# A pairwise-interaction tower in native fp32 row tiles, with half of the groups turned so that the batch lies on the partitions

## What is computed

```python
e = jnp.stack([tbl_0[ids[:, 0]], ..., tbl_31[ids[:, 31]]], axis=1)   # 1024 x 32 x 64
xi, xj = e[:, idx_i, :], e[:, idx_j, :]                              # i < j, 496 pairs
z = jnp.sum(jnp.einsum('bpd,pde->bpe', xi, W) * xj, axis=-1)         # 1024 x 496
h = jnp.concatenate([z, dense_ctx], axis=1)                          # 1024 x 512
h = jnp.maximum(h @ W_top1 + b_top1, 0.0)
h = jnp.maximum(h @ W_top2 + b_top2, 0.0)
y = h @ W_top3
```

## Time and profile before

| | us |
|---|---|
| median of 3 runs (lowest, highest) | 643.97 (643.26, 646.44) |
| span of the profiled execution | 631.3 |
| median less span | 12.7 |
| PE busy | 515.1 (82%) |
| PE weight loads busy | 260.2 (41%) |
| DVE busy | 390.0 (62%) |
| ACT busy | 220.5 (35%) |
| POOL busy | 344.0 (55%) |
| mean granted TensorE clock | 0.935 of full |

### The profile page before, as it was taken

One profiled execution on the slowest core, in us unless ns is written; L12 is line 12 of the kernel. 1 busy time (PEld: TensorE's weight loads), 2 busy tenths in 40 slices (PEclk: granted clock), 3 DMA queues, 4 the chain that ended last, 5 costly groups with the idle time before them and its releaser, 6 DMA issues.

```text
span 631.3 us, 6463 instructions
## 1 busy us (share of the span) xinstructions
PE 515.1 (82%) x2288; PEld 260.2 (41%) x2288; DVE 390.0 (62%) x408; ACT 220.5 (35%) x387; POOL 344.0 (55%) x346
## 2 busy tenths in 40 slices
PE   1324028698899979999993999699799999999998
PEld 0112014244454435455551454344355555555542
DVE  1221026688799976877773135597678887877720
ACT  1621125344443425325142244254344433332003
POOL 7777727466444347678474445658788844332000
PEclk9997558799899999999997899899899999999999
DMA  2131102222322242331110000122223331110000
GB/s 38 34 75 43 27 20 52 43 56 57 58 58 50 53 108 42 65 71 23 29 23 19 18 15 20 37 61 59 54 41 62 67 58 31 35 29 2 1 0 0
DMA packets 72453, 25.77 MB, mean 41 GB/s; under 512 B 67555, under 2 KB 68067, under 8 KB 72421
## 3 DMA queue, kind: packets, MB, share of 16 engines
q1 hardware_dynamic: 63908, 15.91, 13.4%
q0 software_dynamic: 8512, 9.45, 7.3%
HBM read 25.34 MB, written 0.00 MB: 40 GB/s over the span
## 4 chain that ended last, share of the span: by engine, by line
PE 72%; another core or an unknown queue 8%; issue 7%; DVE 5%; POOL 4%; ACT 2%; DMA 1%; DVEq 0%; ACTq 0%
PE z_sum L628 24%; PE left L610 20%; PE left L611 18%; PE left L646 4%; POOL gathered L414 4%; DVE products L480 3%; PE xT L593 2%; PE left L659 2%; DVE x_lo L458 1%; DVE w_split L372 1%; PE left L668 1%; ACT x_hi L514 1%; DMA gathered<-in_tbl_dram,ids_sb 0%; ACT x_hi L507 0%
## 5 line engine op out<-in xcount | busy, mean ns | idle before, releaser
L480 DVE TENSOR_TENSOR products<-left,X 128x1024 f32<-128x1024 f32 x240 | 285.0, 1220 | 131.8 <-remote 63.6
L414 POOL DMA_INDIRECT gathered<-in_tbl_dram,ids_sb x256 | 249.4, 974 | 156.2 <-PE xT L593 79.9
L610 PE MATMUL left<-x_hi,w_split 128*128 128x512 f32 x440 | 186.1, 423 | 5.9 <-DVE products L480 3.9
L628 PE MATMUL z_sum<-products,ones_window 128*32 128x512 f32 x960 | 160.1, 611 | 18.4 <-DVE products L480 10.7
L611 PE MATMUL left<-x_lo,w_split 128*128 128x512 f32 x440 | 174.2, 396 | 0.0
L372 POOL TENSOR_TENSOR w_split<-raw_w,w_split 64x512 fp32r<-64x512 f32 (+5 forms) x78 | 89.0, 1160 | 72.9 <-ACT w_split L529 72.5
L610 PEld LDWEIGHTS left<-x_hi,w_split 128*128 128x128 f32 x440 | 83.5, 190 | 92.7 <-issue 44.6
L529 ACT ACTIVATE w_split<-raw_w 64x512 fp32r<-64x512 f32 (+4 forms) x124 | 65.3, 566 | 72.3 <-PE left L611 68.5
L611 PEld LDWEIGHTS left<-x_lo,w_split 128*128 128x128 f32 x440 | 83.7, 190 | 14.4
L519 ACT ACTIVATE x_lo<-x_lo 64x512 fp32r<-64x512 f32 x64 | 40.3, 629 | 126.6 <-DVE x_lo L458 85.0
L610 PE MATMUL left<-x_hi,w_resident 128*128 128x512 f32 x72 | 37.2, 516 | 57.6 <-ACT x_lo L519 34.0
(11 more groups left out here) (34 smaller groups left out, 135.5 us busy)
## 6 DMA issues: line engine op xcount, KB each, us to landing
gathered<-in_tbl_dram,ids_sb POOLq DMA_INDIRECT x256
raw_w<-in_L_rec_W_dram SPq DMA_DIRECT2D x2, 496.0 KB
raw_w<-in_L_rec_W_dram SPq DMA_DIRECT2D x2, 480.0 KB
raw_w<-in_L_rec_W_dram SPq DMA_DIRECT2D x2, 464.0 KB
raw_w<-in_L_rec_W_dram SPq DMA_DIRECT2D x2, 448.0 KB
raw_w<-in_L_rec_W_dram SPq DMA_DIRECT2D x2, 432.0 KB
raw_w<-in_L_rec_W_dram SPq DMA_DIRECT2D x2, 416.0 KB
raw_w<-in_L_rec_W_dram SPq DMA_DIRECT2D x2, 400.0 KB
```

What stands on the lines that cost most here:

```text
L414: pool.indirect_dma_start(out=gathered[:, g % GATHERS, t, odd, :], out_offset=None, in_=tables[f], in_offset=bass.IndirectOffsetOnAxis(ap= ...
L480: nc.vector.tensor_tensor(products[:, G % PRODS, :, :], left[:, s, :, :], X[:, x_slot(h, k):x_slot(h, k) + 1, :].to_broadcast([P, 2, HB]), ...
L610: nc.tensor.matmul(left[:, s, odd, :], w, x_hi[:, g % X_RING, odd, :], start=True, stop=False)
L628: ins = nc.tensor.matmul(z_sum[32 * q:32 * q + 32, :], window[:, 30 - 2 * t:62 - 2 * t], diagonal[:, h, :] if k == m else products[:, G % ...
```

## The change

It replaces nearly the whole kernel. The layers, the triangle of steps and the window sum are kept.

- **Matmuls.** x and W are no longer split. W is loaded once and stays: the matrices of field 2m lie on partitions 0 to 63 and those of field 2m+1 on 64 to 127 of `w_sb`. A matmul is native fp32 over 64 partitions; the two fields of a step are two row tiles of PE.
- **Quarters.** The batch is worked in four quarters of 256 samples, with x in `X` for two quarters.
- **Two kinds of work.** A "columns" piece holds two groups of 256 samples: four matmuls of 64 x 128 weights and 256 columns, one DVE multiply of 128 x 1024, two window sums. A "rows" piece has x as the stationary operand and W as the moving one: for 128 samples, two matmuls of 512 columns cover four groups k, the batch lies on the output's partitions, DVE multiplies by the gathered rows as they are, and the sum over 64 features is along the free side. By `row_chunks` a quarter has 30 columns pieces, 30 rows pieces, and 2 "own" pieces that hold the diagonals of eight steps each.
- **Row sums.** They are one DVE reduction (`rowsum`), or 16 ACT copies of 64 elements with an accumulator output (`rowsum0`, `rowsum1`), or six halvings on POOL (`poolsum`), into `z_nat`, which PE turns once a quarter (`zT`).
- **Order.** `Order` walks through the work with a table of costs and puts into one list what each engine does next. It gives a row sum to ACT if ACT is free, to POOL if the gathers are over, else to DVE if DVE is free.
- **Gathers.** The same 256 gathers of tables and 4 of the first layer's rows, in four quarters of 64. Gather g waits until a number of pieces have been multiplied (`pieces_before`), and the third and fourth quarter's first until the quarter two before is done.

```diff
-            eng.tensor_tensor(weights(g, i, slice(D, P), cell, pairs), raw_w[:, load % RAW, a:a + pairs, :],
-                              weights(g, i, slice(0, D), cell, pairs).bitcast(F32), ALU.subtract).then_inc(made, 1)
...
-                nc.vector.tensor_tensor(x_lo[at, g % X_RING, odd, :], X[at, x_slot(h, m), :],
-                                        x_hi[at, g % X_RING, odd, :].bitcast(F32),
-                                        ALU.subtract).then_inc(x_lo_natural, 1)
...
-                    nc.tensor.matmul(left[:, s, odd, :], w, x_hi[:, g % X_RING, odd, :], start=True, stop=False)
-                    ins = nc.tensor.matmul(left[:, s, odd, :], w, x_lo[:, g % X_RING, odd, :], start=False, stop=True)
...
+def row_chunks(m):
+
+    return [] if m > 10 else {3: [12, 8], 2: [12, 7], 1: [12, 8], 0: [12, 7]}.get(m, [12])
...
+COLUMN_PRODS = 6
+ROW_PRODS = 5
+
+BATCHES = [2, 2, 2, 1, 1, 1, 1, 2, 2, 2]
+LAST_BATCHES = [2, 2, 2, 2, 2, 2, 2, 2]
...
+GROUP, AHEAD, APART, LAG = 1, 44, 1.02, 3
+FIRST_AHEAD, FIRST_APART = 16, 0.5
...
+def pieces_before(g):
+
+    if g % GROUP:
+        return 0
+    n = int(max((g - AHEAD) * APART, (g - FIRST_AHEAD) * FIRST_APART if g < 4 * FP else 0))
+    if g // 4 - LAG <= FP:
+        n = min(n, WITHIN[max(0, g // 4 - LAG)])
+    return max(0, n)
...
+    def sum_rows(self, now, limit):
+
+
+        gathered = self.landed(QUARTERS - 1, 0)
+        while self.waiting:
+            ready = self.end[self.row_work[self.waiting[0]]] + SIGNAL
+            if max(self.act, ready) <= now + ACT_SLACK:
+                self.by_act(self.waiting.pop(0))
+            elif gathered is not None and max(self.pool, gathered - POOL_AFTER, ready) <= now + ACT_SLACK:
+                self.by_pool(self.waiting.pop(0))
+            elif max(self.dve, ready) + ROWSUM_DVE <= limit + DVE_SLACK:
+                self.by_dve(self.waiting.pop(0))
             else:
+                return
...
+            for m in range(FP - 1, -1, -1):
+                for i in (2 * m, 2 * m + 1):
+                    if i < F - 1:
+                        a, pairs, odd = first_pair(i), F - 1 - i, i % 2
+                        column = w_base(m) + 1 + odd
+                        sp.dma_start(w_sb[D * odd:D * odd + D, column:column + pairs, :],
+                                     W[a:a + pairs].rearrange("p d e -> d p e")).then_inc(w_loaded[m], 16)
...
+                        before = pieces_before(g)
+                        if before:
+
+                            pool.wait_ge(multiplied, before)
...
+            def row_sum(w, o):
+
+                x, n = work[w], rows_before[w]
+                act.wait_ge(multiplied, w + 1)
+                z_nat_free(act, x[1])
+                for j in range(8):
+                    tile, column = x[2] % (2 * QT), 16 * ROW_UNITS.index(x[3:5]) + 8 * o + j
+                    product = row_products[:, n % ROW_PRODS, o, j * D:(j + 1) * D]
+                    ins = nc.scalar.activation(product, product, ACT.Copy, accum_out=z_nat[:, tile, column:column + 1])
...
+                if x[0] == "columns":
+                    for g, (m, k) in enumerate(x[2]):
+                        for odd in (0, 1):
+                            ins = nc.tensor.matmul(left[:, s, odd, QB * g:QB * (g + 1)], weights(odd, m, k, 2),
+                                                   X[D * odd:D * odd + D, q % 2 * FP + m, :], start=True, stop=True)
+                elif x[0] == "rows":
+                    t, m, c = x[2] % QT, x[3], x[4]
+                    for odd in (0, 1):
+                        ins = nc.tensor.matmul(left[:, s, odd, :], X[D * odd:D * odd + D, q % 2 * FP + m, P * t:P * (t + 1)],
+                                               weights(odd, m, c, 8), start=True, stop=True)
+                else:
+
+                    pe.wait_ge(copied, copies["wT", 1 - x[2] // 8])
+                    for g in range(4):
+                        for o in (0, 1):
+                            m, part, to = x[2] + 2 * g + o, slice(D * o, D * o + D), slice(D - D * o, P - D * o)
+                            ins = nc.tensor.matmul(left[to, s, g // 2, g % 2 * QB:(g % 2 + 1) * QB], w_sb[part, w_base(m) + 1, :],
+                                                   X[part, q % 2 * FP + m, :], start=True, stop=True)
+                ins.then_inc(projected, 1)
```

More of the change, by code:

```diff
@@ L91, in fields_to_split @@
[L91 to L128, removed]
@@ L131, in z_row, with pair, w_base, column_groups @@
-def z_row(u):
-    return 32 * (u % 4) + 2 * (u % CHUNK // 4)
+def pair(i, j):
+    return first_pair(i) + j - i - 1
+def w_base(m):
+    return sum(F - 2 * a for a in range(m))
+W_COLUMNS = w_base(FP)
+def row_chunks(m):
+    return [] if m > 10 else {3: [12, 8], 2: [12, 7], 1: [12, 8], 0: [12, 7]}.get(m, [12])
+def column_groups(m):
+    return [k for k in range(m + 1, FP) if not any(c <= k < c + 4 for c in row_chunks(m))]
+ROW_UNITS = [(m, c) for m in range(FP - 1, -1, -1) for c in row_chunks(m)]
@@ L142, in w1_rows @@
-    return index
-def make_plan():
[L148 to L219, removed]
@@ new lines, in make_plan @@
+def make_plan():
+    order = Order()
+    while order.next():
+        pass
+    plan, last = order.plan, QUARTERS - 1
+    if ("zT", last) not in plan:
+        plan.append(("zT", last))
+    plan.append(("early", last))
+    plan += [("sum", v) for v in range(order.sums, SUMS * QUARTERS)]
+    plan += [("layer1", (last, n)) for n in range(4)] + [("layer2", (last, n)) for n in range(2)] + [("layer3", (last, 0))]
+    own = [w for w, x in enumerate(order.work) if x[0] == "own"][:2]
+    for n, w in enumerate(own):
+        plan.insert(plan.index(("work", w - 3)), ("wT", n))
+    return plan, order.work, order.batches
@@ new lines, in dlrm_tower @@
+        x_ready = {(q, m): copies["x", n] for n, (q, fields) in enumerate(batches) for m in fields}
+        columns_before, rows_before = [], []
+        for x in work:
+            n = len(columns_before)
+            columns_before.append(sum(a[0] != "rows" for a in work[:n]))
+            rows_before.append(sum(a[0] == "rows" for a in work[:n]))
+        row_work = [w for w, x in enumerate(work) if x[0] == "rows"]
+        dve_sums = [n for what, n in plan if what == "rowsum"]
+        act_sums = [n for what, n in plan if what == "rowsum1"]
@@ new lines, in dlrm_tower, with wait_row_sums, z_nat_free @@
+        pool_sums = [n for what, n in plan if what == "poolsum"]
+        work_of_quarter = [max(w + 1 for w, x in enumerate(work) if x[1] <= q) for q in range(QUARTERS)]
+        def wait_row_sums(eng, n):
+            last = row_work[n - 1]
+            for by, pieces in ((dve_summed, dve_sums), (act_summed, act_sums), (pool_summed, pool_sums)):
+                done = sum(w <= last for w in pieces)
+                if done:
+                    eng.wait_ge(by, done)
+        def z_nat_free(eng, q):
+            if q >= 2:
+                eng.wait_ge(transposed, copies["zT", q - 2])
@@ L375, in _, with least_field @@
+        def least_field(x):
+            return min(m for m, k in x[2]) if x[0] == "columns" else x[3] if x[0] == "rows" else x[2]
+        block = ctx.enter_context(nc.Block())
         @block.sync
@@ L476, in multiply @@
                     return
[L477 to L489 removed]
+                n = rows_before[w]
```

931 lines of the change are left out of this document (581 added, 350 removed).

## The result

The changed kernel takes 518.61 us (median of 6 runs, 515.25 to 522.34) against 643.39 us (6 runs, 642.2 to 646.44): a ratio of 0.805, 95% interval 0.802 to 0.809. It is faster, as forecast, but 104 us over the forecast of 415 and 49 us over the range.

A forecast was written before the change was run, and what follows sets the result against it. Bound by a gather-paced start, then PE. Forecast: 45 us start, 333 us of PE work at 95% (350) ending at 395, 6 us end, 12.7 to the median: 415 us, range 388 to 470.

The forecast's parts named there:

- gathers cost no more than the first 45 us: Start: eight field pairs landed at 45.5 us, 15 us of PE work done; later quarters' bounds about equal, 378 us.
- binds little: POOL's pacing asks 1.43 us per gather against 1.25, starting 62 us ahead of need; little effect before the last quarter.
- DVE and PE are both under 85% in the middle: Stated sign in the next profile that the order, not a price, is at fault.
- Row tiles overlap: PE, 240 pieces: 0.84 us each side by side, 202 us; rival at 1.68 each gives 624 us, chance 0.07.
- Own pieces go in pairs: PE, 8 own pieces: 1.68 us each, 13 us; rival, serial at 3.36, gives 429 us, chance 0.20.
- A row sum on ACT: 16 copies at 0.25, 4.0 us; upper bound 8.0 if each accumulator output needs another instruction, rival chance 0.05.
- W is hidden: W's 8.1 MB load, some 60 us when sharing, wanted at 85 us: hidden by the gathers at no cost.
- the term: Row sum on DVE: taken as 1.15 us, a multiply's pace, within 0.6 to 1.22.
- the second rival: Level engines wait for each other through product buffers and banks: 85% busy instead of 95%, 456 us, chance 0.11.
- the 95%: PE's busy share after the start, three engines level: 333 us of work takes 350, ending at 395.
- The granted clock: 1.00 from about 60 us on; rival, clock stays at 1.2 GHz, over 700 us if for all work, chance 0.03.
- PE busy: PE's summed work in the changed kernel: 348 us, against 474 for the kernel before by the same prices.

The follow-up runs named there:

- e7: Changed kernel in bursts of 4: only every fourth gather waits for its count of pieces; 425.3 us where the kernel before takes 559.0.
- e4: Changed kernel with ACT's row sums as plain copies without the accumulator output, sums left out; 508.5 us where the kernel before takes 642.9.
- e1: Changed kernel with W's loads spread, each waiting for rows of a later field pair; 520.8 us where the kernel before takes 642.9.
- f2: The probe program of e5, unchanged, on a chip where the kernel before takes 643.2; 545.9 us, one run.
- h2: Changed kernel with a 384-element POOL memset after each gather, 1.55 us apart or more, pace kept; 466.3 us where the kernel before takes 632.8.
- e5: Probe, not the kernel: free-running instruction rows on PE, DVE, ACT beside four phases of 48 gathers at different spacings; 442.4 us, before 559.0.
- e8: Changed kernel in bursts of 16: only every sixteenth gather waits for its count of pieces; 426.2 us where the kernel before takes 559.0.
- g3: Changed kernel with a 256-element memset after each gather, no pace by pieces, order planned for 1.45 us; 459.1 us, before 561.4.

## Why the prediction was wrong

**The step that failed** is the one on POOL and on the start: "gathers cost no more than the first 45 us", and with it that the pacing "binds little". I took POOL as an engine beside the others, whose instructions cost them nothing but the wait for rows; what they do to the others' instructions was put at nothing, without a reason. On the chip of the result, gathers 1.25 us apart hold up every other engine's instructions. The pace breaks such runs up, but only partly. The price of the hold: 425.3 us for the nearest kernel without it against a forecast of 415, 518.6 with it. So some 10 us of the miss are the sum's own and some 93 the hold's. The changed kernel itself wasn't run on a free chip; bursts of 4 differ from it by fewer waits alone, and bursts of 16 took the same there.

**The row I misread** is in the earlier trace rows, 60 to 80 us: PE, DVE and ACT nearly idle under POOL's unbroken gathers, clock 0.50. I called it a start at the pace of the gathers. The same trace speaks against that: POOL was as many steps ahead as it may be, and behind its gather at 82.88 it waited 10 us for PE's transposes (the last line; 79.9 us of such waits over the whole run). What PE waited for, 34 us, was a chain of single instructions on ACT and DVE, with pauses of 9 to 10 us:

```profile
79.88 0.63 ACT L519 ACTIVATE x_lo<-x_lo 64x512 fp32r<-64x512 f32 x1 [10.01 <-DVE x_lo L458]
...
88.53 1.22 DVE L480 TENSOR_TENSOR products<-left,X 128x1024 f32<-128x1024 f32 x1 [8.68 <-remote]
...
90.50 0.63 ACT L519 ACTIVATE x_lo<-x_lo 64x512 fp32r<-64x512 f32 x1 [9.99 <-DVE x_lo L458]
...
91.23 0.76 PE L610 MATMUL left<-x_hi,w_resident 128*128 128x512 f32 x1 [33.99 <-ACT x_lo L519]
...
POOL gathered L414 <- PE xT L593: 79.9, 11, 10.0
```

These lines show waits, not gaps by "issue", so they would have refuted my reading but not named the cause. That the kernel before loses to the hold too (643 us on the one kind of chip, 559 on the other, 84 us) is likely but only argued: it wasn't run with spaced gathers. If so, the forecast's ratio was worse than its time. Where there is no hold, 425.3 us is near 415, but the ratio is 0.76 against the forecast's 415 / 644 = 0.64, because the kernel before is faster there as well.

**The sign that fired and misled.** The prediction wanted the order, not a price, blamed if DVE and PE are both under 85% in the middle. From 80 to 200 us they are (PE 84.4 of 120 us, DVE 70.1). But e7 keeps the order of PE, DVE and ACT and takes 425, so it wasn't the order.

**Right in number.** All but the row sum on ACT are so by their own steps:
- Row tiles overlap. A rows piece takes 1.0 us with its restart, two of them 1.99 here; their four matmuls one after the other would be 3.4:

```profile
308.18 1.99 PE L849 MATMUL left<-w_sb,X 64*128 64x512 f32 x8
310.18 2.39 PE L844 MATMUL left<-X,w_sb 64*128 64x256 f32 x16
```

- Own pieces go in pairs: 16 records in 1.95 us, not 3.4. The Trainium skill, TensorEngine Tiling (Array Packing), Restrictions and Gotchas, says that different row tiles can't access one bank at the same time; the trace doesn't agree, since by that the piece would take twice as long.

```profile
304.43 1.95 PE L857 MATMUL left<-X,w_sb 64*64 64x256 f32 x16 [0.18 <-DVE column_products L688]
```

- A row sum on ACT takes 3.8 us against 4.0 forecast, but by luck. The accumulator output adds an instruction of 189 ns, the upper bound's mechanism; copies with it stand 0.24 us apart. In e4, without it, they stand 0.15 apart (193.0 us for 1280, against 306.8):

```profile
L742 ACT ACTIVATE row_products<-row_products 128x64 f32<-128x64 f32 x1280 | 193.0, 243 | 29.0 <-DVE row_products L697 22.2 <-issue 6.8
```

So it costs some 0.09 us a copy, an estimate of 115 us for all 1280, where the forecast had nothing. The forecast made up for it by taking the copy's duration for its distance from the next, which it had warned of for PE. The copy's 243 ns agree with the 239 that follow from the Trainium skill, ScalarE: Activation LUTs, What ACT_TABLE_LOAD costs. What a kernel without the reads would gain where there is no hold was not run.
- W is hidden (e1, run with the hold only), though the DMA share stands at 1.16 in the first 40 us and the first rows are turned 3.4 us later beside it. DVE's reduction takes 1.21 us, 0.06 over the term.
- The pacing does bind (the last gather starts at 358.7 us in e7, not near 330), but at no cost that shows there.
- The engines don't wait for each other as the second rival has it: from 200 to 380 us in e7 PE is busy 179.6 of 180 us, better than the 95% allowed, with DVE at 91% and ACT at 92%.
- The granted clock is low only where PE rests: 0.74 from 80 to 120 us, 0.96 or more in each window from 200 on, 0.996 over all of e7.

**Off in size, with luck in the sum.** PE busy in e7 is 379 us, not 348: a piece takes 0.9 to 1.1 us from start to start there, not 0.84, which a restart at each wait for a `left` bank would explain (not isolated). The span of e7 is 422.2 us where the forecast has 401, so the sum for the span is 21 us short, not 31: the 95%, where e7 lost next to nothing, took up the rest. Another 10 were hidden by the last term. The 12.7 us added for the distance from span to median are not there: e7's run took 423.95 us with a span of 422.2, the changed kernel's 515.47 with 513.7, and a run of before 645.16 with 643.1, so 1.8 to 2.1 us each. So the 631.3 us of the first table must be the span of a faster execution than those of the median. 415 against 425 is closer than its working deserves.

## What to carry to other kernels

Where GpSimd issues indirect DMAs back to back, look at whether the other engines' instructions with nothing to wait for keep their spacing ("issue" gaps in the middle of a row of equal instructions). If not, keep gathers apart (1.55 us was enough here) and time on more than one chip: the spacing that gained 42 us on one cost 40 on another. An engine that is off the chain of waits can still set everyone's pace; a probe with free-running rows of instructions on each engine shows it in one run.

## What the hardware showed that was not expected

- On chip 1, gathers 1.25 us apart slow ACT and DVE to one instruction in 1.4 us each and PE to 10 records in 32 us (f2). It sets in with a delay: in f2 the first gather starts at 23.5 us and ACT keeps its pace until 31; in the changed kernel a run of gathers starts at 87.0 and ACT keeps its pace in the row sum from 94.6 to 97.2. It ends with a delay too: 8.9 us after the start of the last gather in f2, 4.1 in the changed kernel. At 1.55 us apart it is gone (f2; h2 has a single gap of 1.4 us in its row sums). On chip 10 nothing is seen at any spacing (e5, e7, e8), on chip 0 nothing at 1.44 (g3); closer gathers weren't run there.
- What holds the engines stays open, and so does what sets the chips apart. The profile's two instruction queues moved the same in e5 and f2 (15 packets of 0.25 MB and 29 of 0.24 MB), so it isn't their amount; whether single transfers came late was not looked at. The Trainium skill, SBUF — State Buffer, SBUF: two separate sides, names a port pair that GpSimd and VectorE share, and says that PE and ScalarE never wait on anyone at their ports. Here they are held more than VectorE is, and on some chips alone, so that pair is not the explanation.
